# Attention stages: constants and first loads moved, last sums and their copies spread over the next group

## The reference

```
a: softmax(q k / sqrt(8) - slope_h * |i - j|) v, then @ Wout + bout
b: softmax((q k / sqrt(8)) * exp(-|decay| * |i - j|)) v, then @ out_w.T + out_b
c: xh = layernorm(x) by heads; xc = xh - mean over tokens
   softmax(xc xc) xh
```

## Time and profile before

| | |
|---|---|
| median of 3 runs (lowest, highest) | 3620.84 us (3614.31, 3624.82) |
| profiled execution, its own time | 3614.17 us |
| its span | 3611.5 us |
| busy in the span: PE, DVE, ACT, POOL | 2940.0, 2250.9, 2358.0, 462.7 us |
| mean granted TensorE clock | 0.924 |

### The profile page before, as it was taken

One profiled execution on the slowest core, in us unless ns is written; L12 is line 12 of the kernel. 1 busy time (PEld: TensorE's weight loads), 2 busy tenths in 40 slices (PEclk: granted clock), 3 DMA queues, 4 the chain that ended last, 5 costly groups with the idle time before them and its releaser, 6 DMA issues. The chain is left out here.

```text
span 3611.5 us, 55084 instructions
## 1 busy us (share of the span) xinstructions
PE 2940.0 (81%) x18300; PEld 1335.7 (37%) x18300; DVE 2250.9 (62%) x3797; ACT 2358.0 (65%) x3466; POOL 462.7 (13%) x320
## 2 busy tenths in 40 slices
PE   4588888799997458888879999967878743999997
PEld 2122222566665211111156666622236541111115
DVE  6477777677777746666767777667789865000004
ACT  5589888455443658989945544464633345999993
POOL 5000000000001300000000000035635331000002
PEclk9799999899998779999989999989989966999998
DMA  3444431000000443334200000000000003222210
GB/s 92 66 57 57 56 54 24 24 0 0 0 0 5 118 76 50 44 49 53 36 24 0 0 1 0 0 25 1 0 0 0 0 2 98 40 40 40 40 27 26
DMA packets 78673, 110.84 MB, mean 31 GB/s; under 512 B 11777, under 2 KB 42497, under 8 KB 77649
## 3 DMA queue, kind: packets, MB, share of 16 engines
q1 hardware_dynamic: 78480, 108.32, 18.0%
HBM read 80.59 MB, written 27.69 MB: 30 GB/s over the span
## 5 line engine op out<-in xcount | busy, mean ns | idle before, releaser
L809 ACT ACTIVATE b_direct_probs<-b_direct_s_ps 128x1024 f32<-128x1024 f32 x512 | 473.6, 1095 | 63.2 <-DVE b_direct_s_ps L833 58.6
L1447 ACT ACTIVATE m_mix_hidden<-m_mix_up_ps 128x512 f32<-128x512 f32 x512 | 305.7, 597 | 293.9 <-PE m_mix_up_ps L1391 293.7
L809 ACT ACTIVATE a_direct_probs<-a_direct_s_ps 128x1024 f32<-128x1024 f32 (+10 forms) x512 | 430.1, 940 | 86.4 <-DVE a_direct_s_ps L836 82.7
L809 ACT ACTIVATE c_att_probs<-c_att_s_ps 128x1024 f32<-128x1024 f32 x512 | 470.2, 1166 | 15.9 <-PE c_att_s_ps L746 13.7
L1399 PE MATMUL m_mix_down_ps<-m_w,m_mix_hidden 128*128 128x128 f32 x4096 | 474.8, 276 | 0.0
L1399 PEld LDWEIGHTS m_mix_down_ps<-m_w,m_mix_hidden 128*128 128x128 f32 x4096 | 467.2, 192 | 15.3 <-issue 15.3
L1391 PE MATMUL m_mix_up_ps<-m_mix_ZT,m_w 128*128 128x512 f32 x1024 | 470.4, 617 | 0.0
L833 DVE TENSOR_TENSOR b_direct_s_ps<-b_direct_s_ps,b_distance 128x512 f32<-128x512 f32 x512 | 333.0, 695 | 171.8 <-PE b_direct_s_ps L746 171.8
L836 DVE SCALAR_TENSOR_TENSOR a_direct_s_ps<-a_distance,a_slopes,a_direct_s_ps 128x512 f32<-128x512 f32 (+3 forms) x512 | 352.8, 732 | 140.0 <-PE a_direct_s_ps L746 138.1
L822 DVE COPY c_out_t<-c_att_o_ps 128x512 f32 x32 | 20.6, 686 | 477.0 <-PE c_att_o_ps L765 477.0
L765 PE MATMUL b_direct_o_ps<-b_direct_probs,b_v_cols 128*32 128x512 f32 x2048 | 279.5, 624 | 3.8 <-ACT b_direct_probs L809 3.8
(11 more groups left out here) (343 smaller groups left out, 3623.7 us busy)
## 6 DMA issues: line engine op xcount, KB each, us to landing
qk_parts<-b_qkv_parts SPq DMA_DIRECT2D x96, 128.0 KB, 2.4
qk_parts<-a_qkv_parts SPq DMA_DIRECT2D x48, 128.0 KB, 2.4
a_k_rows<-qk_parts SPq DMA_DIRECT2D x32, 192.0 KB
a_q_rows<-qk_parts SPq DMA_DIRECT2D x32, 192.0 KB
b_k_rows<-qk_parts SPq DMA_DIRECT2D x32, 192.0 KB
b_q_rows<-qk_parts SPq DMA_DIRECT2D x32, 192.0 KB
qk_parts<-c_split_parts SPq DMA_DIRECT2D x24, 256.0 KB, 3.6
c_k_rows<-qk_parts SPq DMA_DIRECT2D x32, 192.0 KB
```

The lines of the kernel that those rows point to most:

```text
L809: act.activation(probs[:, J % 2, j, lo:hi], s_ps[:, slot(hg, n), lo:hi], ACT.Exp).then_inc(exped, 1)
L1447: act.activation(hidden[:, f, :], up_ps[:, f % UP_BANKS, :], ACT.Silu).then_inc(silu_done, 1)
```

## The change

- **Constants.** A class `Constants` takes the place of `Distances` and `BiasRows`. Its work runs in the first block, while X is read: POOL counts distances, ACT takes their absolute value, DVE makes slopes, the rows of ones, the cleared `v_cols` with its column of ones, and the bias pieces, and SP stores these in 7 DMAs and waits for them. b reuses distances and `v_cols`.
- **No clearing.** The score matmuls read only the rows that hold data (48, and 54 in the tile with the bias of a, 49 in c), so `q_rows` and `k_rows` are not cleared. c's row of ones is loaded with two more DMAs for each group. c's `v_cols` is cleared by POOL in `centre_and_split`.
- **First load.** `Operands.load` issues a group's DMAs. SP calls it for the first group at the end of `project_qkv` and `centre_and_split`, behind the wait for the last store. `bound_scores` becomes the end of `project_qkv`'s lists for DVE and PE.
- **Last sums and copies.** The right sums of a group's last J move behind the scores of unit 4 of the next group, as for every other J. The two copies are made one by one: the left half behind adjust 4 (its sums count in `left_summed`), the right half behind adjust 7. A group's first left sums wait for the left copy alone, its first right sums for the right one. In c DVE does nothing else and copies each half as its sums are done.

```diff
 class Operands:
-    def clear(self, pool, shift_rows=False):
-        pool.memset(self.q_rows[:].bitcast(F32), 0.0).then_inc(self.cleared, 1)
-        pool.memset(self.k_rows[:].bitcast(F32), 0.0).then_inc(self.cleared, 1)
-        pool.memset(self.v_cols[:], 0.0).then_inc(self.cleared, 1)
...
+    def depth(self, tile):
+        if self.shift_dram is not None:
+            return ROWS + 1
+        return ROWS + 6 * (tile == 1 and self.bias_dram is not None)
+
+    def load(self, sp, hg, b):
...
+                sp.dma_start(self.k_rows[row:row + 1, half, :, :],
+                             self.ones_dram.unsqueeze(0)[:, hs, :]).then_inc(loaded, 16)
...
 project_qkv, sync:
             for b in range(RING):
                 sp.wait_ge(stored[b], 16 * 3 * (SPLITS // RING))
+            operands.load(sp, 0, 0)
 attend_transposed:
+    TAKE_AT = (4, 7)
...
-                    rows = slice(PAIR_ROW * tile, PAIR_ROW * (tile + 1))
+                    rows = slice(PAIR_ROW * tile, PAIR_ROW * tile + operands.depth(tile))
...
             def sum_up(hg, J, c, b):
+                if J == 0:
+                    pe.wait_ge(o_out, b * (2 * HG) + (2 * hg + 3 + c))
                 if c == 0:
                     if J == 0:
-                        pe.wait_ge(o_out, b * (2 * HG) + (2 * hg + 4))
...
                         if n % GH == GH - 1:
                             sum_up(hg, n // GH, 0, b)
-                            if n + 1 == UNITS:
-                                sum_up(hg, n // GH, 1, b)
-                        if n % GH == 1 and n > GH:
-                            sum_up(hg, n // GH - 1, 1, b)
+                        if n % GH == 1:
+                            if n > GH:
+                                sum_up(hg, n // GH - 1, 1, b)
+                            elif hg:
+                                sum_up(hg - 1, JT - 1, 1, b)
+                            elif not first:
+                                sum_up(HG - 1, JT - 1, 1, b - 1)
...
                         adjust(b, hg, n)
-                        if n == SLOTS - 1:
+                        if n in TAKE_AT:
+                            c = TAKE_AT.index(n)
                             if hg:
-                                take_sums(b, hg - 1)
+                                take_sums(b, hg - 1, c)
...
+class Constants:
+    def take(self, act):
+        act.wait_ge(self.counted, 3)
+        act.activation(self.distance[:, :], self.distance[:, :].bitcast(I32), ACT.Abs)
+
+    def make(self, dve, ident, ident_ready):
+        link = counter(dve, self.made)
+        for h, s in enumerate(alibi_slopes()):
+            last = dve.memset(self.slopes[:, h:h + 1], -s)
+        link(last)
+        link(dve.memset(self.rows[:, 3, :], 1.0))
+        link(dve.memset(self.v_cols[:], 0.0))
+        link(dve.memset(self.v_cols[:, :, :, :, HD:HD + 1], 1.0))
+        dve.wait_ge(ident_ready, 2)
+        link(dve.tensor_tensor(self.diagonal[:, :], self.slopes[0:HEADS, :], ident[0:HEADS, 0:HEADS], ALU.mult))
+        link(dve.tensor_reduce(self.slope_of[:, :], self.diagonal[:, :], AX, ALU.add))
+        dve.wait_ge(self.counted, 2)
+        link(dve.tensor_copy(self.away[:, :], self.away[:, :].bitcast(I32)))
+        link(dve.tensor_scalar(self.size[:, :], self.away[0:HEADS, :], self.slope_of[:, 0:1], None, ALU.mult))
...
+    def keep(self, sp):
+        sp.wait_ge(self.made, self.steps)
+        sp.dma_start(self.bias_dram[3:6].rearrange("r h t -> h r t"), self.rows[:, 0:3, :]).then_inc(self.kept, 16)
+        for row in (0, 1, 2, 6, 7, 8):
+            sp.dma_start(self.bias_dram[row], self.rows[:, 3, :]).then_inc(self.kept, 16)
+        sp.wait_ge(self.kept, 16 * 7)
...
 centre_and_split:
+        @block.gpsimd
+        def _(pool):
+            pool.memset(operands.v_cols[:], 0.0).then_inc(v_cleared, 1)
```

More of the change, by code:

```diff
@@ L719, in _, with ahead @@
+            def ahead(b, hg):
+                sp.wait_ge(o_out, b * (2 * HG) + (2 * hg + 2))
+                operands.load(sp, hg % HG, b + hg // HG)
+            with sp.Fori(0, BATCH - 1) as b:
+                for hg in range(1, HG + 1):
+                    ahead(b, hg)
+            for hg in range(1, HG):
+                ahead(BATCH - 1, hg)
         @block.gpsimd
```

341 lines of the change are left out of this document (155 added, 186 removed).

## The result

The changed kernel takes 3533.76 us (median of 4 runs, 3525.11 to 3535.8), the kernel before 3620.11 beside it (4 runs): a ratio of 0.9758, 95% interval 0.9736 to 0.9779. Forecast were 3527, with 3500 to 3560. The profiled execution took 3535.8 us (span 3534.1), the slowest of its four; span against span the gain is 77.4 us, median against median 86.4.

What follows compares the result with a forecast made beforehand. ACT's exponentials pace all three attentions, held up in a and b until DVE has adjusted the scores. Terms summed to -90.7 us, giving 3523.5 from the profiled execution and 3530 from the median; forecast 3527, range 3500 to 3560.

Steps and rivals of the forecast that it cites:

- layer norm b: Layer norm of b: with POOL empty the standard deviation comes 9.6 us earlier and ACT's Abs goes, -11.3 us.
- first load a, b, c: Start of each attention: load issued right behind the stores, first score earlier by 7.9 and 7.6 us, c -0.5.
- attention of a: Group boundaries of a: -6.6 us for wide heads, 3 for entering narrow ones, 3.4 for the clock, -13 in all.
- attention of c: Boundaries of c: ACT's 2.2 us of idle time, all put down to sums in one piece, would go, -2.2.
- the last copies: Ends of a, b and c: one copy at each runs under the last sums, -1.8 us.
- a scaling of 2.12: Layer norm of c: a 128x8 DVE scaling taking 2.12 us had waited with POOL clearing beside it; the term was -11.2.
- The walk through the queues: Boundaries of b: exponential 8 late by 0.95 us instead of exponential 3 by 1.78, gain 0.83 fifteen times, -12.5.
- The load that "leaves 1" us: Attention of a: SP's next load, now behind the right copy, takes 18.5 us and still arrives with 1 us to spare.
- PE waiting for a DMA at a group's start: Start of a group in attention: a sign that would prove the prediction wrong; no size given.
- The free handover: Boundaries of b and a: DVE reaches the right copy before PE asks, another -25 us, 3502 total; chance 0.15.
- rival 2: Boundaries: new wait as long as the old, clock falls as often, 3567, or 3548 in half form; chance 0.21 together.
- The pairs of 48 rows: Score matmuls: with 48 rows for 64 a pair no longer runs side by side, 3840 us total; chance 0.04.

Runs made afterwards that it cites:

- the kernel with the late load: Changed kernel with each stage's first load issued behind the branch again, the bound's chain left where the change put it: 3538.3 us, ratio 0.978.
- the spreading alone: Kernel before with only the later last sums, copies at units 4 and 7 and PE's loop of the change, old fronts: 3575.66 us, ratio 0.9899.
- the fronts alone: Changed kernel with last sums in one piece at a group's end, both copies at unit 2, PE's old loop: 3578.16 us, ratio 0.9882.
- the three with POOL's work in b: Changed kernel with POOL work back beside b's layer norm: memsets 3530.43 us; iotas ahead of them 3536.13; the old seven instructions, first six without waits, 3531.09.

## Why the prediction was right, point by point

The time came out 7 us above the forecast of 3527 and inside the range, and the main mechanisms, an idle POOL in the layer norms and the spread sums and copies in b, did what the prediction said. But some terms hit by luck, and two missed. Term by term, forecast and measured (profiled executions):

| Term | Forecast | Measured | From |
|---|---|---|---|
| front of the program | +5.5 | +4.2 | first reduction 11.73, then 15.88 |
| layer norm a | -15.2 | -15.4 | 37.99 to 22.54 until the projection |
| layer norm b | -11.3 | -11.9 | 39.00 to 27.11 |
| layer norm c | -11.2 | -11.8 | 38.72 to 26.94, to the first matmul of the split |
| first load a, b, c | -7.9, -7.6, -0.5 | -7.2, -8.2, 0.0 | first score after the last store |
| attention of b | -25.5 | -26.0 | 514.87 to 488.84 |
| attention of a | -13 | -5.7 | 495.16 to 489.50 |
| attention of c | -2.2 | +1.9 | 472.74 to 474.64 |

Together -80.1, where the terms forecast were -88.9 without the last copies; the span shows -77.4, since what stands between these rows took 2.7 us more. 2.3 of that lie behind c's last exponential, where the prediction had a gain: the last copies (-1.8) were not read by themselves, but no gain of theirs shows at the end of a, b or c.

**Layer norms.** The sizes are right, to within 0.6 us. The reason for b is only half shown: the removal freed DVE, whose first scaling took 10.03 us before and 0.17 after, and with ACT's Abs of 1.81 that makes nearly all of the 11.9; but the same POOL instructions put back cost 1.7 to 2.0 us and not 10. So it is shown that the time went with the new fronts, and not that POOL's work by itself is worth it. For c it was not a scaling of 2.12, but eight scalings that took 15.07 us while POOL wrote rows of ones for 13.93, a row that I did not look for. The Trainium skill (SBUF — State Buffer, "Who interferes with whom") says that whoever starts first holds the port pair for a whole instruction. The rows with POOL's work put back agree (3.42 us beside a memset of 3.53); the 10.03 of before lasts through four instructions of POOL and is not covered by it.

**First loads.** The sum was right partly by luck. In a the load starts 7.2 us earlier behind the last store, close to the 6.9 that I had, and from its start to the first score it takes 21.3 us as before. I had taken the branch at 5.0 us, and so the second load as beginning 11.8 us into the first, for a gain of 1.0 more. The branch took 13.3 us, so the first load ran alone: 19.8 us until its last packets, instead of the 18.5 that I took and the 20.1 that I got with the second beside it. And the reason for the earlier start was in the main another: issuing the load ahead of the branch brings 2.0 us in a and 1.9 in b. The other 5.2 and 6.3 came with what the kernel with the late load keeps: the bound's chain under the stores, which I had put at 1.8 and no gain of its own, and SP's first load, which does not wait for DVE any more. In a the flag is read 2.1 us sooner behind the last store, and the load then starts 3.2 us sooner behind the flag.

**Boundaries of b.** The walk through the queues held: PE waits 0.87 (0.95), a group takes 30.17 (30.28), the right copy ends at 6.96 (7.0), and the clock comes back (I took 13 of 16, and nearly all of it came: 0.99). Moving the copy one unit earlier returned the rest. What the walk did not have is the turn of DVE's loop, 1.3 us at two batch ends. It is no part of the spreading: with the spreading alone it isn't there, and with the fronts alone it is.

**a.** The term was -13 and this execution shows -5.7, so it missed here; but one execution doesn't size it. The attention of a has the same program in four kernels, the changed one and the three with POOL's work in b; it took 489.5, 483.8, 486.6 and 480.6 us there, and 481.9 with the spreading alone. The forecast of 482 is at the edge of that scatter. Two steps of the prediction were wrong. The load that "leaves 1" us was late in all four (PE waits 2.20 in the changed kernel, 0.66, 0.23 and 1.54 in the others): this is the sign "PE waiting for a DMA at a group's start", which was to prove me wrong, and for a it did. And the clock was to come back by 3.4, but PE's only loop turn now falls into a's narrow group 8: PE idles 1.98 to 2.43 us there in all four kernels, and the group takes 31.7 to 33.6 us (33.38 at 0.74 here). Written out it took 28.67, so 3 to 5 us of it are the loop's.

**c.** Wrong in sign, by 4 us. The 2.2 us of ACT's idle time were there, but not at the sums in one piece, to which I gave all of it: a group inside a batch takes 29.33 for 29.35. They lay in the first group and at the three batch ends (0.59 idle at each), where numbering the score buffers through took them away. New costs came on top: group 8, with PE's loop turn, takes 30.70 for 29.11, and the first group half a microsecond more.

**The rivals.** The free handover (3502) did not come with this change, but it is what one number makes of it: 3503.57. The spreading did what it says, so rival 2 is out. The pairs of 48 rows are not slower: in the page's rows of b the score matmuls average 390 ns, for 401 before, and in c, where the clock did not fall in either, 390 in both. That fits the tiles of 64 rows that the Trainium skill lists (TensorEngine Tiling (Array Packing), "Tiling Modes").

## What to carry to other kernels

Walk the queues at a boundary with the trace's own durations, and ask for each piece moved what it next stands in front of: the walk gave the stall left (0.87 us a group), and moving one copy one unit earlier was worth 28 us more. When a stall goes, read what is left at each group: a buffer numbering that starts anew with each batch and loads with 1 us to spare showed only then. A loop's turn can grow with a change elsewhere in the kernel (DVE's took 2.8 us for 0.3), so read it again after each change. Before a term is credited to a row, undo that part alone: two terms here were right in size for a reason that held only in part.

## What the runs showed of the hardware

- The code behind a branch is fetched by DMA and waits behind a load in flight: 13.3 us from flag to ACT's first instruction in a with a load of 14 DMAs issued ahead of it, 4.3 without; 12.2 and 3.3 in b with 12 DMAs.
- PE was at half pace right behind an idle stretch of 2.31 us in some places (8 sum matmuls in 1.93 us, 16 in 1.92 just before) and at full pace in others: of b's 15 boundaries in the kernel before, 8 show 1.06 or 1.07 us for 8. With idle times of 0.87 to 0.90 all 15 do.
- The turn of DVE's loop in b's attention, from the branch to the next instruction, took 0.3 us in the kernel before and with the spreading alone, 2.8 in the changed kernel and 3.0 with the fronts alone.
- Six small stores took 7.03 us to issue while the read of X was in flight, and 2.73 behind it.
- POOL's work in one piece held a DVE scaling of 128x8 for 10.03 us in the kernel before and 10.02 with the spreading alone; in another kernel the same instructions on other memory let it in after 1.36.
- DVE's clearing of v_cols took 1.76 us. By the Trainium skill (VectorE: DVE Perf Modes, "Zero memsets can be issued as uint32 (trn2)") I had an estimated 2.1; the row stands.
